# Half of the first output product's depth moved into the tiles of the graph attention, with the stores on GpSimd's queue and two score tiles loaded in the stage before

## The reference, cut to what matters

```python
# graph attention (GAT), 21250 edges and self loops, 4 heads of 64
xl, xr = down @ Wl, down @ Wr                    # down = rmsnorm(xn) @ W_down
e = sum(att * leaky_relu(xl[src] + xr[dst]))     # one score per edge and head
alpha = softmax of e over the edges of a target
gat = segment_sum(alpha * xl[src], dst) @ W_up
# mix
mixed = q (k^T v) z                              # 1250 x 1024
x = x + gat + mixed @ Wo.T + bo                  # "the output product" is mixed @ Wo.T
y = layernorm(x); prob = y @ gate_w              # goes on into the experts
```

## Time and profile before

| what | value |
|---|---|
| median of 3 runs | 2940.43 us (2932.8 to 2944.59) |
| span of the profiled execution | 2940.1 us, which is also the only time that the page gives for it |
| PE busy | 2668.4 us, 91% |
| DVE, ACT, POOL busy | 55%, 33%, 27% |
| mean granted TensorE clock | 0.952 |

### The profile page before, as it was taken

The page is one execution under the profiler, slowest core; times in us unless marked ns, Lnnn a source line. Parts: engine busy times, 40 slices in busy tenths (PEclk is TensorE's granted clock), DMA queues, the critical chain, the costliest instruction groups (busy, mean ns, idle before and its releaser), DMA issues. The chain is left out here.

```text
span 2940.1 us, 51469 instructions
## 1 busy us (share of the span) xinstructions
PE 2668.4 (91%) x19570; PEld 2513.2 (85%) x19570; DVE 1606.8 (55%) x3190; ACT 961.0 (33%) x1941; POOL 791.7 (27%) x772
## 2 busy tenths in 40 slices
PE   6677899999885998699979999999999999999788
PEld 6455799999885997588869999899998999999577
DVE  7677677787634886655553222254545332225655
ACT  4466433333203563244431010243434120001243
POOL 0567766777640332122200000000000001100054
PEclk9888999999996998799989999999999999999989
DMA  8933433433739882477753111121112653224382
GB/s 242 289 100 110 115 114 96 116 100 82 209 104 212 225 202 97 117 184 202 193 123 107 40 36 52 30 61 31 58 34 91 185 159 93 65 63 122 121 280 75
DMA packets 202069, 362.93 MB, mean 123 GB/s; under 512 B 33654, under 2 KB 135246, under 8 KB 200595
## 3 DMA queue, kind: packets, MB, share of 16 engines
q1 hardware_dynamic: 165733, 278.89, 32.5%
q0 software_dynamic: 36112, 80.96, 10.9%
HBM read 272.97 MB, written 98.15 MB: 126 GB/s over the span
## 5 line engine op out<-in xcount | busy, mean ns | idle before, releaser
L180 PE MATMUL mix_bank<-sums_w_hi,layer_act_hi 128*125 128x256 f32 x1280 | 359.9, 281 | 0.0
L181 PE MATMUL mix_bank<-sums_w_lo,layer_act_hi 128*125 128x256 f32 x1280 | 359.2, 281 | 0.0
L182 PE MATMUL mix_bank<-sums_w_hi,layer_act_lo 128*125 128x256 f32 x1280 | 358.7, 280 | 0.0
L3184 POOL TENSOR_TENSOR sage_add<-sage_add,sage_bias 125x256 f32<-125x256 f32 x40 | 29.4, 736 | 1193.1 <-DMA sage_add<-resid 1192.9
L181 PEld LDWEIGHTS mix_bank<-sums_w_lo,layer_act_hi 128*125 128x125 f32 x1280 | 237.8, 186 | 0.2
L182 PEld LDWEIGHTS mix_bank<-sums_w_hi,layer_act_lo 128*125 128x125 f32 x1280 | 237.9, 186 | 0.0
L180 PEld LDWEIGHTS mix_bank<-sums_w_hi,layer_act_hi 128*125 128x125 f32 x1280 | 237.7, 186 | 0.1
L567 POOL DMA_INDIRECT scored_ring<-xl,edge_idx x168 | 176.6, 1051 | 157.5 <-issue 138.2
L574 POOL DMA_INDIRECT scores<-edge_e,edge_idx x168 | 174.6, 1039 | 138.5 <-DMA scores<-edge_e,edge_idx 98.9
L567 POOL DMA_INDIRECT scored_ring<-xr,edge_idx x168 | 172.6, 1027 | 51.6 <-issue 51.0
L924 PE MATMUL count_pa<-count_hot_s,count_hot_d 125*125 125x416 bf16 (+1 forms) x624 | 137.5, 383 | 29.9 <-DVE count_hot_s L834 27.8
(11 more groups left out here) (638 smaller groups left out, 8575.0 us busy)
## 6 DMA issues: line engine op xcount, KB each, us to landing
ffn_raw<-in_L_ffn_w_dram SPq DMA_DIRECT2D x16, 2048.0 KB, 13.0
scores<-targets_hole SPq DMA_DIRECT2D x40, 546.9 KB
ffn_raw<-in_L_ffn_W_dram SPq DMA_DIRECT2D x16, 1024.0 KB
gat_sc<-scores SPq DMA_DIRECT2D x6, 2187.5 KB
lasting_raw<-in_L_mix_w_qkv_dram SPq DMA_DIRECT2D x24, 512.0 KB, 3.9
scored_ring<-scores SPq DMA_DIRECT2D x4, 2187.5 KB
layer_slab<-in_L_gnn_W_neigh_dram SPq DMA_DIRECT2D x7, 1024.0 KB
layer_slab<-in_L_gnn_W_self_dram SPq DMA_DIRECT2D x7, 1024.0 KB
```

Source lines behind the costliest of these rows:

```text
L180: pe.matmul(out, lhs[0], rhs[0], start=first, stop=False)
L181: pe.matmul(out, lhs[0], rhs[1], start=False, stop=False)
L182: return pe.matmul(out, lhs[1], rhs[0], start=False, stop=last)
L3184: pool.tensor_tensor(add[:, u % 2, :], add[:, u % 2, :], bb[:, g * SLAB:(g + 1) * SLAB], ALU.add) \
```

## The change

It has five parts. The output product is cut in its depth: out0 keeps pieces 0 to 3 (NEAR = 4), and pieces 4 to 7 (FAR = 4) are computed in gat for each tile, as 2 x 4 x 3 matmuls of 128x512 at the head of `product`, into the bank that takes the W_up product; the `idle` matmuls go. For that gat loads 512 columns of Wo whole (2.1 MB) at its start and turns and splits them in eight rounds, each PE, ACT, DVE in turn through the bank `pr`, placed between the work of tile 0; per tile it loads 256 KB of the mixed rows (`far`), rounded by ACT, the rest taken by GpSimd (`mix_rest`). mix0 stores slabs 4 to 7 in the layout of `far`. In out0 the chunks of Wo are two in place of four per slab, the last quotient of mix0 moves into slab 1, and two parts of `mixt` are loaded in mix0 already. Two edge batches move from out0 into count (COUNT_BATCHES = 26). FirstScores loads two tiles, before both stores of slab 3. gat has two score buffers, `wgt` has two heads in place of four, and its stores of x and y are issued by GpSimd.

```diff
-COUNT_BATCHES = 24
+COUNT_BATCHES = 26
-DEEP = 3
+DEEP = 2
...
     def load(self, sp, edges):
         edges.landed(sp)
-        move_rows(sp, self.ring[0:R, 0:N * HEADS], self.rows, self.s_in)
+        move_rows(sp, self.ring[0:R, 0:N * HEADS], self.rows[0], self.s_in)
+        move_rows(sp, self.second[:, :, :].rearrange("p s h -> p (s h)"), self.rows[1], self.s_next)
...
# gat, SP
-                tile(0)
+                counts_of(0)
                 move_rows(sp, rows_x, xl.rearrange("(t p) c -> p t c", p=R)[:, :, 0:HID], s_x)
+                sp.dma_start(wide_raw[:, :, :], wo.rearrange("(i p) k -> p i k", p=P)[:, :, NEAR * P:D]).then_inc(s_wide, 16)
...
+                for t in range(T - DEEP):
+                    scores_of(t + DEEP)
+                    mixed(t + DEEP)
+                    rows(t + DEEP)
+                    counts_of(t + DEEP)
...
# gat, POOL, at the end of each tile
                     if t + 1 < T:
                         biased(t + 1)
+                    store(t)
+                    if t + 1 < T:
+                        mix_rest(t + 1)
                     norm.deviation(pool, t)
+                    if t:
+                        norm.store(pool, t - 1)
...
# gat, DVE
                 first_maxima()
                 loop_counts(0)
+                far_rest(0)
                 for t in range(T + 3):
                     weigh(t, 0)
+                    if t == 0:
+                        far_rest(1)
...
                     weigh(t, 1)
+                    if t == 0:
+                        far_rest(2, 3)
...
                     weigh(t, 2)
+                    if t == 0:
+                        far_rest(4, 5)
...
                     weigh(t, 3)
+                    if t + 1 < T:
+                        loop_counts(t + 1)
                     if t == 0:
+                        far_rest(6, 7)
...
# gat, PE
                 def product(t, c):
+                    cols = slice(c * BANK, (c + 1) * BANK)
                     pe.wait_ge(s_lo, t + 1)
                     if c:
                         pe.wait_ge(s_held, 2 * t + 1)
+                    else:
+                        pe.wait_ge(s_mlo, t + 1)
+                    for k in range(FAR):
+                        mm3(pe, pr[0:R, :], [x[:, t % 2, k, :] for x in mix], [x[:, k, cols] for x in w_far], k == 0, False)
...
-                    if 1 <= t < T:
-                        idle(16)
...
-                    if 1 <= t < T:
-                        idle(10)
...
# out0, SP
+                    if first is not None and g == 2:
+                        sp.wait_ge(s_quot, NC)
+                        sp.dma_start(far_part(far, SLABS - 1), output.last.rearrange("p (t r) -> p t r", r=R)).then_inc(s_far, 16)
+                    if first is not None and g == NSLAB - 1:
+                        first.load(sp, edges)
                     cols = slice(g * SLAB, (g + 1) * SLAB)
                     for half in range(2):
...
-                        if first is not None and g == NSLAB - 1 and half:
-                            first.load(sp, edges)
...
# out0, DVE
-                for _ in range(2):
-                    if todo is not None:
-                        todo.step()
-                for k in range(begun, KD):
-                    if todo is not None and k in (1, 4, 7):
-                        todo.step()
+                for k in range(begun, KS):
                     dve.wait_ge(s_phi, k + 1)
...
+                    if todo is not None:
+                        todo.step()
...
-                        if todo is not None and i in ((5, 9), (1, 4, 6, 9), (1, 4, 6, 9), (2, 5, 8))[g] and todo.left():
+                        if todo is not None and i in (1, 3, 5, 7) and todo.left():
                             todo.step()
...
# out0, PE
-                        for k in range(KD):
-                            ins = part_product(g, t, k, k == 0, k == KD - 1)
+                        for k in range(KS):
+                            ins = part_product(g, t, k, k == 0, k == KS - 1)
```

More of the change, by code:

```diff
@@ L1057, in keep, with gat_phase @@
         dve.tensor_reduce(self.prob[:, n, :], every, AX.X, ALU.add).then_inc(self.s_prob, 1)
-def gat_phase(nc, first, scores, at, xl, ident, w_up, bias, part, dst, normed, gate_w, prob_out):
+def gat_phase(nc, first, scores, at, xl, ident, w_up, wo, bias, part, far, dst, normed, gate_w, prob_out):
     with Phase(nc, "gat") as ph:
-        sc = [first.tile] + [ph.sb(f"sc{i}", [R, N, HEADS], F32) for i in range(1, DEEP)]
+        sc = [first.tile, first.second]
         cnt = ph.sb("cnt", [R, DEEP, T, R], F32)
@@ L1928, with __init__ @@
 class OutputSlabs:
-    QUARTERS = 4
-    def __init__(self, ph, wo, flip, ahead):
+    def __init__(self, ph, wo, flip, ahead, room=None):
         self.wo, self.flip, self.ahead = wo, flip, ahead
-        self.parts = [ph.sb(f"part{i}", [P, N], F32) for i in range(ahead)]
+        self.depth, self.chunks = (NEAR, 2) if flip else (KD, 4)
+        lent = [] if room is None else [room[:, 0:N], room[:, N:2 * N]]
+        self.parts = [ph.sb(f"part{i}", [P, N], F32) for i in range(ahead - len(lent))] + lent
         self.s_parts = ph.sems("part", ahead)
@@ L1958, in load_parts, with output_phase @@
             sp.dma_start(self.parts[k][:, :], mixt[k * P:(k + 1) * P, :]).then_inc(self.s_parts[k], 16)
-def output_phase(nc, name, act_hi, act_lo, mixt, output, ident, resid, dst, edges=None, turn=None, load=None, room=None, run=None, stage=0, first=None, near=None):
-    WC = OutputSlabs.QUARTERS
+def output_phase(nc, name, act_hi, act_lo, mixt, output, ident, resid, dst, edges=None, turn=None, load=None, run=None, stage=0, first=None, near=None, far=None):
+    WC, KS = output.chunks, output.depth
     DEEP = 4
@@ L1973, in output_phase @@
     with Phase(nc, name, run) as ph:
-        part = output.parts + ([room[:, 0:N], room[:, N:2 * N]] if room is not None else [])
-        part += [ph.sb(f"part{i}", [P, N], F32) for i in range(len(part), DEEP)]
-        w = [output.w0, [ph.sb(f"w1_{s}", [P, KD, SLAB], F32R) for s in ("hi", "lo")]]
+        part = output.parts + [ph.sb(f"part{i}", [P, N], F32) for i in range(output.ahead, DEEP)]
+        w = [output.w0, [x[:, NEAR:KD, :] for x in output.w0] if flip else
+             [ph.sb(f"w1_{s}", [P, KS, SLAB], F32R) for s in ("hi", "lo")]]
+        if first is not None:
+            first.open()
         res = ph.sb("res", [R, 2, T, SLAB], F32)
@@ L1988, in whole_part @@
         def whole_part(k):
[L1989 removed]
+            return part[k % DEEP][:, :] if flip or k < KD - 1 else output.last
         def chunk(c, h):
             if flip:
[L1994 removed]
                 return wide[c % NC][:, :].rearrange("p (k n) -> p k n", n=P), \
[L1996 removed]
+                    [x[:, 0:NEAR, c * P:(c + 1) * P] for x in w[h]]
             return output.quarter(c, w[h])
@@ L2024, in _ @@
                     run.enter(sp, stage)
-                for k in range(output.ahead, KD - 1):
+                for k in range(output.ahead, KS if flip else KD - 1):
                     if k >= DEEP:
@@ L2052, in _ @@
                     sp.wait_ge(s_st[h], LANDED * NSLAB)
+                if far is not None:
+                    sp.wait_ge(s_far, 16)
             @block.gpsimd
```

230 lines of the change are left out of this document (154 added, 76 removed).

## The result

The changed kernel takes 2992.57 us in the median (2987.05 to 2999.02, 4 runs), the kernel before 2942.51 us (2932.8 to 2953.21, 4 runs with the three of above). The ratio is 1.0165, 95% interval 1.0133 to 1.0196; in a second session it was 1.0178 (1.0150 to 1.0205) with a median of 2992.55. The change costs 50 us; 2987 was forecast, in a range from 2960 to 3006. The profiled execution took 2992.54 us at a span of 2990.8.

What follows compares the result with a forecast made beforehand. The edge chain on POOL was taken to end only 8.5 us before out0's product, with PE bounding gat's middle tiles. The terms 8 (gat starts later), 10 (gat's start) and 29 (tiles) sum to 47, 2987 us; range 2960 to 3006.

Steps and rivals of the forecast that it cites:

- What binds out0: End of out0: the scatters set it, PE done 6 us before them; gat's first DMA near 910.5, 8 us later.
- The last scatter within 5 us of 883: Sign to look for at out0's end: the scatter chain on POOL still ends near its old place, 883 us.
- I take 3 us: Edge chain: moving two batches into count brings the last scatter 3 us earlier, to about 882; bounds 0 and 19.0 us.
- gat's start: From gat's first DMA to the first turned result: 10 us later through Wo's load and eight rounds; bounds 0 and 15.
- The tiles: gat's tiles: far matmuls in, idle matmuls out, 29 us more in all, each tile 21.4 + 2.7 = 24.1 us.
- The bound of 36: Upper bound of the 29 us for gat's tiles, reached if the last tiles run at the low clock.
- The gap at the change of stage: Between out0 and gat: loads ahead of slab 3's stores make gat start 8 us later; bounds 11 earlier, 14 later.
- The sign of the idle matmuls: gat's tiles: taking 26 idle matmuls out of each of nine saves 2.9 us per tile, in all 26.4.
- POOL's lock-out: Rival in gat's tiles: POOL's issues and mix_rest each wait 2.76 us for DVE, 22 us more, 3009; chance 0.08.
- out0 follows PE: Rival, faster: out0 ends with PE's product, needing the last scatter near 828, 57 us earlier; -12, 2928; chance 0.04.
- The starts pay: Rival, same: stores ahead of the loads (-11) and Wo's rounds hidden in gat's start (-8); +10, 2950; chance 0.08.
- A score tile late in every tile: Case in gat's tiles: each score load comes late for DVE, total over 3010; chance 0.03.

Runs made afterwards that it cites:

- round0_later: The changed kernel with the first round of Wo moved behind the first head's multiplication on PE, ACT and DVE: 2994.88 us, 1.0181 of the kernel before.
- stores_first: The changed kernel with slab 3's stores issued ahead of the two score tiles: 2994.81 us, 1.0181 of the kernel before.
- gat_sp_stores: The changed kernel with the graph attention's stores issued by SP again, among its loads: 3086.10 us, 1.0496 of the kernel before.
- after_best: The changed kernel with slab 3's stores ahead of the score tiles and Wo's first round behind the first multiplication: 2987.24 us, 1.0161 of the kernel before.
- after: The changed kernel as it is, against the kernel before: 2992.57 us, ratio 1.0165.

## Why the prediction was right, and where it was off

**What binds out0** was right: the scatters, and not PE, decide when gat starts, PE was done 4 us before the last was issued (6 forecast), and SP's order did what was said: loads, then stores, then S 29.8 us behind the first load (28.5 forecast, from 882 to 910.5). "The last scatter within 5 us of 883" failed: 872.5. The step that failed is "I take 3 us" for the two batches in count. The mean over thirteen profiles has 7 us, in this program 10.5; the opened wait of 10.0 us was not eaten by the later ones as argued: POOL's gathers waited for DVE 9.2 us from 150 to 743 us, where it had been 19.0. At the start of the tail the gain was even 15.7 us (its thirteenth scatter from the end left at 830.64, before at 846.32, and DVE's last edge step began at 831.5 where "near 846" was forecast); the tail itself then took 41.9 us instead of 36.7. The text also reads POOL as issuing "one DMA after the other" outside those waits. That leaves out the 52.0 us that scatters waited for the landing of the one before in the same stretch of the kernel before. mix0's delay, put at 4.5 us, is 4.6 in the means. This term is off by 6 us in the sum, and by some 3 against the mean S of five kernels with the changed order (907.7, where 910.5 was forecast).

**gat's start** was right in size and in kind: 11.2 us for 10. far_rest(0) delayed the first multiplication as said (end S + 22; forecast S + 24), Wo had landed when PE turned it at 922.4, S + 18.0 (19.5), and the first turned result came at S + 61.3 (59 to 60). round0_later shows that about 4 us of it are DVE's order, stores_first that Wo's landing moves with the order of the loads and that a chain of fixed length (40.6 us from the first remainder to the first quotient) follows it.

**The tiles** were right where they are steady, 2.74 us more each for a forecast 2.7, PE busy 217.8 of 220.8 us, but the whole is 34.1 us for 29. The term that was mis-sized is the first tile: 25.5 us instead of 19.4, at a granted clock of 0.84 where the kernel before had 1.00 in the same place. It is 25.4 to 26.8 us in all kernels with the far matmuls. The bound of 36 had this ("if the last tiles run at the low clock") at the wrong end of the stage. What follows the last turned result took 6.2 us more for 5.6.

**The sum was closer than its terms.** In the profile 50.7 us more stand against 47. The gap at the change of stage came 5.9 us under its term, gat's start 1.2 over, tiles and last product 5.1 over and the rest of the program 3.3 over. That S and the tiles missed in opposite directions is luck. The range has a small slip too: its upper bounds sum to 65, and it uses 66.

**The sign of the idle matmuls.** The sum counted their removal as 2.9 us of gain per tile. In this sum that is exact, because the far matmuls keep PE without gaps. As a statement on the kernel before it is wrong: alone, the removal costs 12.6 us.

**The rivals.** POOL's lock-out fell: its issues took 0.56 and 0.58 us each beside a DVE that was busy for 72% of the time, `mix_rest` 1.26, and only the power, as before, was held to 2.5 us. POOL's work grew by 2.8 us per tile, where 5 had been taken. The Trainium skill's rule ("SBUF — State Buffer", section "SBUF: two separate sides"), that DMAs issued by GpSimd can stall on DVE's use of the shared ports, did not show in the issue times of these plain stores. gat_sp_stores tells nothing on it, since its tile is bound by the loads. "out0 follows PE" was priced at 2928; with the tail of scatters cut by 37 us the total falls by 9, since SP's order and PE's own dependence on the gathers come next; a last scatter near 828 would hardly have been enough. "The starts pay" has both its pieces in after_best. It was priced at 2950, 37 us under the forecast, with the first result 19 us earlier than in the kernel before (-11 and -8). after_best is 5 us under the changed kernel. Its S does come 17.9 us earlier than before's, but its first quotient 8.1 us later (959.55 against 951.46), where the changed kernel has 13.3 later: an earlier S only moves the loads behind it, and the rounds of Wo take the place of the lost 16.66 us wait. "A score tile late in every tile" did not happen, and gat_sp_stores shows what prevents it.

**The rest of the program** was 3.3 us longer in the profile. It ranges from 1771 to 1779 us over all these kernels, whose code there is the same, and was left at nothing rightly.

## What to carry to other kernels

Before an engine's work is halved, ask what ends the stage besides it, and by how much: here three things (the scatter chain, SP's queue order, PE) ended within 10 us of each other, and PE itself waited through DVE for the gathers, so taking away 57 us of PE work there gave nothing, while the same work cost its full price where PE was the bound. A queue that mixes loads with stores that wait for results turns a two-deep buffer into a one-deep one: move one of the two to another queue, or keep the third buffer, as the kernel before did. And an idle filler on PE is not free time to be claimed: count what the clock does without it.

## What the runs showed of the hardware

- TensorE's granted clock was 1.00 with PE busy without a wait, in tiles of 21.96 us; 0.93 to 0.76 where it waited about 2 us per tile for DVE; 0.81 where it was busy 105.8 of 147 us. These are means over a tile of the two levels, 2.4 and 1.2 GHz (1.00 and 0.50; in stores_first it was 0.50 from 878 to 893 us, with PE idle since 870). The Trainium skill says the same in kind ("TensorE: Matmul & The Clock Gate", section "Part 1: The HAM clock gate (the "warmup" mystery)"), that an idle PE drops to half rate. That it happens inside an otherwise busy stage, and not in every tile (21.19 us at 1.00 and 23.19 at 0.93 in turn), is from these rows.
- One program repeated the place of its last scatter within 1.5 us (two profiles), while programs with the same edge code differ in it by up to 13.7. A difference of less than that between two kernels, ahead of gat, can't be put down to the edit on the total alone; the profile must show it relative to a point that both share.
- The tail of scatters, each issued when the one before has landed, stood 3.06 us apart in the mean before, with waits of 1.4 to 3.3 us; in after it is 3.5 us, with waits of 1.4 us at the end and of up to 7.4 us while slab 2's stores went out (852.22). Such a chain has no fixed price per link.
